# Two transformer blocks on one core: Q and K copied whole from their banks in attention, a loop of four sequences per round, residual and bias summed in TensorE's output bank in the mixer, and row gathers six experts ahead

## The chip, the cores and the metric

The kernel runs on one core of a Trainium2 chip. The time is the device time of one launch in microseconds. A core has TensorE (PE in the profile; it writes only to banks of PSUM), VectorE (DVE), ScalarE (ACT), GpSimd (POOL) and SyncE (SP), each with its own instruction queue, which wait for each other by semaphores; DMAs are issued from SP, ACT and POOL queues.

## What is computed

Sixteen sequences of 512 tokens with 128 channels go through two blocks. The part of the reference that matters:

```python
x = x + _L0_attn_ref(_layernorm(x), W_attn, W_proj)     # 16 heads of 8, causal, ALiBi, softmax
x = x + _L0_ffn_ref(_layernorm(x), ...)                 # expert choice: 8 experts take 256 tokens each
x = x + _L1_attn_ref(_layernorm(x), ...)                # the mixer, below
x = x + _L1_ffn_ref(_layernorm(x), ...)                 # top 2 of 8 experts of width 352

# _L0_attn_ref
scores = jnp.einsum('bhqd,bhkd->bhqk', q, k) * scale + bias
att = jax.nn.softmax(scores, axis=-1)
y = jnp.einsum('bhqk,bhkd->bhqd', att, v)

# _L1_attn_ref (mixer): residual is its own, normalised, input
uv = x @ in_proj_w + in_proj_b
v_local = _dwconv(silu(v), conv_w, conv_b)
h = a * h + ssm_b * vt                                  # a scan over the sequence
out = (u * silu(y_seq)) @ out_proj_w + out_proj_b
h = out + residual
return (h - mu) * rsqrt(var + LN_EPS) * ln_w + ln_b
```

## The kernel before

The stages follow one another: attention, its projection with the router (project), the choice of tokens (choose), expert choice, the mixer, the gate of the second feed-forward part with its dispatch, and the experts. The change touches attention, expert choice and the mixer.

**Attention.** One round of the loop handles one sequence b in four steps `st`, one for each group of four heads. All engines run the same sequence of rounds: two unrolled, a hardware loop (`Fori`) whose body holds two rounds, two unrolled (`steps`, L235 to L248). In a step TensorE follows the list `ORDER`. S0 to S5 are score products for the row maxima (L436 mask, L441 product), into two PSUM pairs `psS`, from which VectorE takes maxima (`mx`, L548); then VectorE splits the maxima in two bf16 parts `mhl` (L556, L558), TensorE turns them (M, L476), ScalarE copies them to `mT` (L574), and SyncE's DMA puts them into `qop` (L283). E0 to E5 are the score products again, with the maxima inside, for the step two before (L455), twelve units into a ring of three banks `psE`; ScalarE takes the exponential of each (`probs`, L619), GpSimd clears the future part (L344). V0 to V3 multiply by the values (L467) into `psY`, which ScalarE copies (`ysb`, L600).

Into these steps the preparation of the next sequence is woven: transposes of its normalised x (X, L379) at step 0, the products for Q and K (L384) in step 0 and for V (W, L387) in step 2, each into the next bank of the same ring (`RING`). Q and K are needed as three bf16 parts that add up to the f32 value. ScalarE writes the high part from the bank (`hi_part`, L582), VectorE subtracts it from the bank into `rest` (`split`, L514), and GpSimd makes the middle and the low part from `rest` (`split_rest`, L335, L337). A bank with Q or K is free for its next use when `rest` is done:

```python
elif kind_ in "QK":
    eng.wait_ge(s_rst, 2 * bb + 3 + (kind_ == "K"))
```

The parts go to HBM (SyncE) and come back spread over partitions into `qop` and `kop` (`place_q`, `place_k`, L223 and L229, from GpSimd's queue).

**Expert choice.** For each of eight experts GpSimd gathers 256 rows with two indirect DMAs (L1142), TensorE turns them (L1191), and goes through two layers (L1204, L1216); VectorE makes the contribution `ctr`, which GpSimd adds to x in HBM with two indirect DMAs (L1157), each pair after the pair before has landed.

**Mixer.** A skewed pipeline over sequences, written with steps s: ScalarE normalises x of s to `xn` (L1463), TensorE turns it (L1435), then multiplies for V and U (L1440, L1443); VectorE does the taps of the convolution (`tap`, L1550) and the scan (L1579) of s-1 and the product `z` (L1592); for b = s-2 TensorE multiplies z by `wout` into `psO` (L1428), GpSimd has made `xo` = `xn` + bias (L1407), VectorE adds both to `ho` (L1560) and takes its statistics (L1566). The chain of eight small operations (L1512 to L1522) serves x of s+1 and h of s-2 together, GpSimd raises to the power -1/2 and makes `shift` (L1384, L1386), and ScalarE writes `hn` from `ho` (L1493).

## Time and profile before

| | us |
|---|---|
| runs, median (lowest to highest of 3) | 1696.02 (1693.43 to 1698.18) |
| profiled execution | 1699.34 |
| its span in the trace | 1697.4 |
| attention, 40 to 690 | 650 |
| expert choice, 870 to 948 | 78 |
| mixer, 948 to 1132 | 184 |

The last three are stretches of the trace, cut by hand where the stage's first and last operations stand. A line of a timeline gives start, duration, engine, line of the kernel, operation, output and input, and in brackets the idle time before it and what ended it.

### The profile page before, as it was taken

The page shows a single profiled execution, that of the slowest core. Times are in us where ns is not written, and L with a number is a line of the kernel's source. Part 1 is how long each engine was busy: PE and PEld are TensorE (multiplying, and loading weights), DVE is VectorE, ACT ScalarE, POOL GpSimd, SP SyncE. Part 2 cuts the span into 40 slices and gives each one's busy share as a digit, 9 for nine tenths or more (in the row PEclk, how much of TensorE's full clock was granted, in tenths as well). Part 3 has the DMA queues.
Part 4 walks back from the last instruction along what each step waited for, and adds up shares of the span by engine and source line. Part 5 has one row for each costly group of instructions (what it writes and reads, how often), then busy time and mean ns, then how long its engine had stood idle before and what let it go on. Part 6 is the DMA issues. An engine that isn't in the chain of part 4 may idle for free. (4 is left out here: it accounts for less than half of the span.)

```text
span 1697.4 us, 34915 instructions
## 1 busy us (share of the span) xinstructions
PE 1208.6 (71%) x9400; PEld 720.5 (42%) x9403; DVE 1140.5 (67%) x3202; ACT 824.4 (49%) x2033; POOL 966.2 (57%) x1007
## 2 busy tenths in 40 slices
PE   2788787888777888585037266617279899899997
PEld 1333333433333433275036033307246565555655
DVE  2878687777766778286743289867766676666664
ACT  1577676666655767111312266633334444444443
POOL 1465465555454653242016388967157777787777
PEclk7899999999989999565558565555579999999999
DMA  4433243333322431362014300300413333333333
GB/s 106 152 83 97 70 110 91 90 88 86 84 68 79 100 101 64 103 219 95 0 57 97 69 25 25 127 7 25 179 28 42 40 41 41 40 41 42 41 40 39
DMA packets 87021, 124.46 MB, mean 73 GB/s; under 512 B 22050, under 2 KB 57826, under 8 KB 82834
## 3 DMA queue, kind: packets, MB, share of 16 engines
q0 software_dynamic: 39712, 44.13, 16.5%
q1 hardware_dynamic: 39170, 65.92, 11.8%
q10 hardware_dynamic: 8032, 12.93, 2.1%
q8 instruction: 73, 1.20, 0.3%
q14 instruction: 34, 0.28, 0.1%
HBM read 65.23 MB, written 57.16 MB: 72 GB/s over the span
## 5 line engine op out<-in xcount | busy, mean ns | idle before, releaser
L548 DVE TENSOR_REDUCE mx<-psS 128x2 f32<-128x768 f32 (+3 forms) x384 | 386.4, 1042 | 164.0 <-PE psS L441 163.5
L619 ACT ACTIVATE probs<-psE 128x512 f32<-128x512 f32 (+2 forms) x768 | 344.6, 523 | 157.5 <-PE psE L455 156.1
L344 POOL TENSOR_SCALAR_AFFINE_SELECT probs<-probs 128x512 f32<-128x512 f32 x256 | 162.3, 643 | 255.0 <-ACT probs L619 254.9
L2038 POOL DMA_INDIRECT out<-ex_y,ex_idx x136 | 219.2, 1612 | 59.0 <-issue 33.8
L455 PE MATMUL psE<-qop,kop 63*128 63x512 bf16 (+3 forms) x1024 | 194.2, 309 | 75.0 <-DVE rest L514 34.8
L467 PE MATMUL psY<-probs,vaug 128*32 128x512 f32 (+3 forms) x2048 | 178.8, 460 | 9.0 <-POOL probs L344 9.0
L2029 POOL DMA_INDIRECT ex_xg<-expert_tab,ex_idx x136 | 134.1, 986 | 60.8 <-issue 38.7
L2096 PE MATMUL ex_psY<-ah_w3s,ex_hT 128*128 (+1 forms) x816 | 127.4, 293 | 26.3 <-DVE ex_y L2022 24.0
L441 PE MATMUL psS<-kop,qop 61*128 61x128 bf16 (+3 forms) x1024 | 140.0, 307 | 0.0
L455 PEld LDWEIGHTS psE<-qop,kop 63*128 63x128 bf16 x1024 | 64.7, 95 | 155.9 <-ACT probs L619 90.5
L436 PE MATMUL psS<-maskq,spread 64*128 64x128 bf16 (+2 forms) x1536 | 114.0, 225 | 21.3 <-DVE mx L548 20.9
L2106 ACT ACTIVATE ex_hT<-ex_psH 128x256 f32<-128x256 f32 x136 | 52.1, 383 | 157.9 <-PE ex_psH L2072 157.9
L2096 PEld LDWEIGHTS ex_psY<-ah_w3s,ex_hT 128*128 128x128 f32 (+1 forms) x816 | 105.3, 196 | 44.2 <-issue 42.7
L436 PEld LDWEIGHTS psS<-maskq,spread 64*128 64x128 bf16 x1536 | 56.6, 96 | 125.1 <-DVE mx L548 88.1
L2078 PE MATMUL ex_psU<-ah_w1s,ex_xT 128*128 x272 | 108.5, 482 | 0.5 <-ACT ex_xT L2117 0.5
L2022 DVE COPY ex_y<-ex_psY 128x128 f32<-128x128 f32 x136 | 39.7, 292 | 100.2 <-issue 51.9
L2079 PE MATMUL ex_psG<-ah_w2s,ex_xT 128*128 x272 | 106.9, 476 | 0.0
L2008 DVE SCALAR_TENSOR_TENSOR ex_h<-ex_psG,ex_w,ex_up 128x352 f32<-128x352 f32 x136 | 79.3, 583 | 38.6 <-ACT ex_w L2113 25.9
L467 PEld LDWEIGHTS psY<-probs,vaug 128*32 128x32 f32 x2048 | 68.1, 113 | 62.5 <-issue 31.2
L2117 ACT ACTIVATE ex_xT<-ex_psX 128x128 f32<-128x128 f32 x136 | 37.7, 277 | 75.8 <-PE ex_psX L2065 73.5
L2072 PE MATMUL ex_psH<-ident,ex_h 128*128 128x128 f32 (+1 forms) x408 | 71.1, 284 | 0.9 <-DVE ex_h L2008 0.9
L1142 POOL DMA_INDIRECT ec_xg<-norm_tab,idx x16 | 15.7, 982 | 93.0 <-POOLq L896 88.5
(318 smaller groups left out, 2549.7 us busy)
## 6 DMA issues: line engine op xcount, KB each, us to landing
y_scr<-ysb SPq DMA_DIRECT2D x64, 256.0 KB, 2.8
qkv_scr<-parts SPq DMA_DIRECT2D x32, 384.0 KB, 3.2
qop<-qkv_scr POOLq DMA_DIRECT2D x30, 192.0 KB, 4.5
kop<-qkv_scr POOLq DMA_DIRECT2D x30, 192.0 KB, 5.6
expert_tab<-table_rows SPq DMA_DIRECT2D x1, 4352.0 KB, 13.5
pj_num<-y_scr SPq DMA_DIRECT2D x16, 256.0 KB
pj_rec<-rec_scr SPq DMA_DIRECT2D x16, 256.0 KB
x_scr<-x_all ACTq DMA_DIRECT2D x16, 256.0 KB, 3.4
```

The costliest lines, as they stand in the source:

```text
L344: pool.affine_select(diag, diag, [[0, HG], [1, P]], ALU.is_ge, 0.0, base=0, channel_multiplier=-1).then_inc(s_msk, 1)
L436: pe.matmul(out[:, :, P * j + lo:w], spread[rows, lo // HALF], maskq[rows, 0:nh, 0:P - lo], start=(lo == 0), stop=False, skip_group_check= ...
L441: mm = pe.matmul(out[:, h, :], half(qop[n], p, ROW_MAX)[:, hh, P * j:P * j + P], half(kop[n], p, ROW_MAX)[:, hh, 0:w], start=False, stop=( ...
L455: mm = pe.matmul(ring_bank(st, u)[:, W[j] * h:W[j] * h + W[j]], half(kop[m], p, ROW_END)[:, hh, P * j:P * j + P], half(qop[m], p, ROW_END) ...
L467: mm = pe.matmul(psY[32 * h:32 * h + 32, P * k:T], vaug[m_v][:, k, HG * e_v + h, :], probs[e_v % 2][k][:, h, :], start=(k == 0), stop=(k = ...
L548: dve.tensor_reduce(out, src, AX, ALU.max).then_inc(s_su, 1)
L619: act.activation(probs[st % 2][j][:, 2 * p + h0:2 * p + h0 + nh, :].rearrange("p h q -> p (h q)"), ring_bank(st, k)[:, 0:nh * W[j]], ACT.E ...
L2029: pool.indirect_dma_start(xg[t % 4][:], None, ytab, bass.IndirectOffsetOnAxis(ap=idx[t % 8][:], axis=0))\
L2038: pool.indirect_dma_start(out, bass.IndirectOffsetOnAxis(ap=idx[t % 8][:], axis=0), y[m][:], None, compute_op=ALU.add).then_inc(s_sc[m], 16)
L2078: pe.matmul(psU[n][:, 0:DE], xT[n][:], flat(w1s[:, e, :]), start=True, stop=True).then_inc(s_g2, 1)
L2079: pe.matmul(psG[n][:, 0:DE], xT[n][:], flat(w2s[:, e, :]), start=True, stop=True).then_inc(s_g, 1)
L2096: i = pe.matmul(psY[:, 0:C], hT[m][0:wd, f], flat(w3s[0:wd, f, e, :]), start=(f == 0), stop=(f == len(FC) - 1))
```

## The change

In attention ScalarE copies Q and K as f32 from the bank into `rest` (`copy_raw`), and the bank is free with that copy (`s_raw`). VectorE then makes the high part from `rest` in SBUF and subtracts it in place. The order within a step changes: M behind E0, V2 and V3 behind E2, Q's product ahead of S2; ScalarE copies `mT` after its second exponential, `ysb` after its sixth; GpSimd makes K's parts later in its step. The loop body holds four rounds in place of two. In expert choice the first six pairs of gathers are issued at once. In the mixer TensorE puts bias (a bf16 product of ones with three bias parts) and residual (`xn` by the unit matrix) into the bank `psO` before z's product is added there; `xo`, `ho` and their additions are gone, and VectorE's statistics and ScalarE's `hn` read the bank.

The core of the diff:

```diff
-        ORDER = ["S0", "E0", "S1", "E1", "M", "V2", "V3", "S2", "E2", "S3", "E3", "S4", "E4", "S5", "E5", "V0", "V1"]
+        ORDER = ["S0", "E0", "M", "S1", "E1", "S2", "E2", "V2", "V3", "S3", "E3", "S4", "E4", "S5", "E5", "V0", "V1"]
...
-                        eng.wait_ge(s_rst, 2 * bb + 3 + (kind_ == "K"))
+                        eng.wait_ge(s_raw, 2 * bb + 3 + (kind_ == "K"))
-            eng.wait_ge(s_rst, 2)
+            eng.wait_ge(s_raw, 2)
...
-            with eng.Fori(1, nb // 2 - 1) as i:
-                for n in range(2):
-                    body(n, 2 * i + n, False)
+            with eng.Fori(0, (nb - 4) // 4) as i:
+                for k in range(4):
+                    body(k % 2, 4 * i + 2 + k, False)
...
-                pool.wait_ge(s_rst, 2 * b + s + 1)
+                pool.wait_ge(s_rst, 4 * b + 2 * s + 2)
...
                     if st == 1 and more:
-                        for k in range(2):
-                            split_rest(b + 1, k)
+                        split_rest(b + 1, 0)
...
                     for j in range(TT):
+                        if st == 1 and more and j == 2:
+                            split_rest(b + 1, 1)
...
-                        if what == "S3" and st == 0 and not last:
+                        if what == "S2" and st == 0 and not last:
...
-            def split(b, s, bank):
-                dve.wait_ge(s_hi, 2 * b + s + 1)
-                if not isinstance(b, int) or b:
-                    dve.wait_ge(s_lo, 2 * b + s - 1)
-                dve.tensor_tensor(rest[s][:], bank[:], parts[s][:, 0], ALU.subtract).then_inc(s_rst, 1)
+            def split(b, s):
+                dve.wait_ge(s_raw, 2 * b + s + 1)
+                if isinstance(b, int) and b == 1:
+                    dve.wait_ge(s_head, 48)
+                elif not isinstance(b, int) or b:
+                    dve.wait_ge(s_pw[s], 16 * b - 16)
+                dve.tensor_copy(parts[s][:, 0], rest[s][:]).then_inc(s_rst, 1)
+                dve.wait_ge(s_rst, 4 * b + 2 * s + 1)
+                dve.tensor_tensor(rest[s][:], rest[s][:], parts[s][:, 0], ALU.subtract).then_inc(s_rst, 1)
             for s in range(2):
-                split(0, s, psE[s])
-                dve.wait_ge(s_rst, s + 1)
+                split(0, s)
+                dve.wait_ge(s_rst, 2 * s + 2)
...
-                if st == 1 and not last:
-                    split(b + 1, 1, ring_bank(0, "K"))
...
                     if k == 3 and st == 0 and not last:
-                        split(b + 1, 0, ring_bank(0, "Q"))
+                        split(b + 1, 0)
+                    if k == 2 and st == 1 and not last:
+                        split(b + 1, 1)
...
-            def hi_part(b, s, use, bank):
+            def copy_raw(b, s, use, bank):
-                if isinstance(b, int) and b == 1:
-                    act.wait_ge(s_head, 48)
-                elif not isinstance(b, int) or b:
-                    act.wait_ge(s_pw[s], 16 * b - 16)
-                act.activation(parts[s][:, 0], bank[:], ACT.Copy).then_inc(s_hi, 1)
+                if not isinstance(b, int) or b:
+                    act.wait_ge(s_lo, 2 * b + s - 1)
+                act.activation(rest[s][:], bank[:], ACT.Copy).then_inc(s_raw, 1)
...
                                        ring_bank(st, k)[:, 0:nh * W[j]], ACT.Exp).then_inc(s_ex, 1)
-                    if k == 3:
-                        if there(G * b + st - 1):
-                            copy_max(b, st, last)
-                        if there(u) and there(u - 1):
-                            copy_y(u - 1, st + 1)
-                    if k == 5 and ahead:
-                        hi_part(b + 1, 0, use_next(b, 1), ring_bank(0, "Q"))
+                    if k == 1 and there(G * b + st - 1):
+                        copy_max(b, st, last)
+                    if k == 3 and ahead:
+                        copy_raw(b + 1, 0, use_next(b, 1), ring_bank(0, "Q"))
+                    if k == 5 and there(u) and there(u - 1):
+                        copy_y(u - 1, st + 1)
                     if k == 9 and ahead:
-                        hi_part(b + 1, 1, use_next(b, 2), ring_bank(0, "K"))
+                        copy_raw(b + 1, 1, use_next(b, 2), ring_bank(0, "K"))
...
-            for e in range(3):
-                gather(e)
+            def gather_next(e):
+                if 3 <= e < E:
+                    pool.wait_ge(s_xg[e % 3], 32 * (e // 3))
+                if e < E:
+                    gather(e)
+            for e in range(AHEAD):
+                gather_next(e)
             for e in range(E):
-                if e + 3 < E:
-                    pool.wait_ge(s_xg[e % 3], 32 * (e // 3 + 1))
-                    gather(e + 3)
+                if e:
+                    gather_next(e + AHEAD - 1)
...
-                if live(s, nb):
-                    pool.wait_ge(s_xn, s + 1)
-                    if not isinstance(s, int) or s >= 2:
-                        pool.wait_ge(s_h, s - 1)
-                    pool.tensor_tensor(xo[n][:], xn[n][:], rows_s[:, 0], ALU.add).then_inc(s_xo, 1)
...
                     pe.wait_ge(s_z, b + 1)
-                    if not isinstance(b, int) or b >= 2:
-                        pe.wait_ge(s_h, b - 1)
                     for t in range(TT):
-                        i = pe.matmul(psO[n][:, P * t:P * t + P], z[n][:, P * t:P * t + P], wout_s[:], start=True, stop=True)
+                        i = pe.matmul(psO[n][:, P * t:P * t + P], z[n][:, P * t:P * t + P], wout_s[:], start=False, stop=(t == TT - 1),
+                                      skip_group_check=True)
                     i.then_inc(s_o, 1)
+                if live(s - 1, nb):
+                    r = s - 1
+                    if isinstance(r, int) and r == 0:
+                        pe.wait_ge(s_bias, 9)
+                    if not isinstance(r, int) or r >= 2:
+                        pe.wait_ge(s_hn, r - 1)
+                    pe.matmul(psO[1 - n][:], ones[:], bias3[:], start=True, stop=False, skip_group_check=True)
+                    for t in range(TT):
+                        i = pe.matmul(psO[1 - n][:, P * t:P * t + P], ident[:], xn[1 - n][:, t], start=False, stop=False, skip_group_check=True)
+                    i.then_inc(s_open, 1)
...
-                        i = act.activation(hn[n][:, t], ho[n][:, t], ACT.Identity, bias=shift[:, u:u + 1], scale=rstd[:, u:u + 1])
+                        i = act.activation(hn[n][:, t], psO[n][:, P * t:P * t + P], ACT.Identity, bias=shift[:, u:u + 1], scale=rstd[:, u:u + 1])
...
+            row = rows_s[0:BROWS, 0].rearrange("p t c -> p (t c)")
+            dve.memset(ones[:], 1.0).then_inc(s_bias, 1)
+            dve.memset(bias3[:], 0.0).then_inc(s_bias, 1)
+            dve.tensor_copy(biashi[:], row).then_inc(s_bias, 1)
+            dve.wait_ge(s_bias, 3)
+            dve.tensor_tensor(biasrest[0][:], row, biashi[:], ALU.subtract).then_inc(s_bias, 1)
+            dve.tensor_copy(bias3[0:1], row[0:1]).then_inc(s_bias, 1)
+            dve.wait_ge(s_bias, 5)
+            dve.tensor_copy(biasmid[:], biasrest[0][:]).then_inc(s_bias, 1)
+            dve.tensor_copy(bias3[32:33], biasrest[0][32:33]).then_inc(s_bias, 1)
+            dve.wait_ge(s_bias, 7)
+            dve.tensor_tensor(biasrest[1][:], biasrest[0][:], biasmid[:], ALU.subtract).then_inc(s_bias, 1)
+            dve.wait_ge(s_bias, 8)
+            dve.tensor_copy(bias3[64:65], biasrest[1][64:65]).then_inc(s_bias, 1)
...
                 if live(s - 2, nb):
-                    b = s - 2
-                    dve.wait_ge(s_o, b + 1)
-                    dve.wait_ge(s_xo, b + 1)
-                    if not isinstance(b, int) or b >= 2:
-                        dve.wait_ge(s_hn, b - 1)
-                    dve.tensor_tensor(ho[n][:], psO[n][:].rearrange("p (t c) -> p t c", t=TT), xo[n][:], ALU.add).then_inc(s_h, 1)
-                tap(2)
-                if live(s - 2, nb):
-                    dve.wait_ge(s_h, s - 1)
+                    dve.wait_ge(s_o, s - 1)
                     for t in range(TT):
-                        i = dve.bn_stats(stats[:, TT + t], ho[n][:, t])
+                        i = dve.bn_stats(stats[:, TT + t], psO[n][:, P * t:P * t + P])
                     i.then_inc(s_hs, 1)
+                tap(2)
```

How the order moves, at three places. First, attention's second round, step 0, on TensorE, from E0 on (L455 or L456 is E, L476 or L477 is M, L436/L437 with L441/L442 is S, L384/L385 is Q's product, L467/L468 V2 and V3). Before:

```order
L455 MATMUL psE<-qop,kop 128x512 x2
L436 MATMUL psS<-maskq,spread 128x2x128 x2
L436 MATMUL psS<-maskq,spread 128x2x64 x2
L441 MATMUL psS<-kop,qop 128x256 x4
L455 MATMUL psE<-qop,kop 128x512 x2
L476 MATMUL psE<-identb,mhl 8x128 x4
L467 MATMUL psY<-probs_2,vaug 32x256 x4
L467 MATMUL psY<-probs_3,vaug 32x128 x4
L436 MATMUL psS<-maskq,spread 128x128 x2
```

Now:

```order
L456 MATMUL psE<-qop,kop 128x512 x2
L477 MATMUL psE<-identb,mhl 8x128 x4
L437 MATMUL psS<-maskq,spread 128x2x128 x2
L437 MATMUL psS<-maskq,spread 128x2x64 x2
L442 MATMUL psS<-kop,qop 128x256 x4
L456 MATMUL psE<-qop,kop 128x512 x2
L385 MATMUL psE<-xT,wT 128x512
L437 MATMUL psS<-maskq,spread 128x128 x2
L437 MATMUL psS<-maskq,spread 128x64 x2
L442 MATMUL psS<-kop,qop 128x384 x2
L456 MATMUL psE<-qop,kop 128x384 x2
L468 MATMUL psY<-probs_2,vaug 32x256 x4
```

M moved ahead of S1 and E1, Q's product ahead of S2, V2 and V3 behind E2.

VectorE in steps 0 and 1 of the same round (L548 or L551 takes maxima, L556/L558 or L561/L563 make `mhl`, L514, or L517 with L519, is the split). Before:

```order
L548 TENSOR_REDUCE mx<-psS 128x4 x2
L548 TENSOR_REDUCE mx<-psS 128x2 x2
L514 TENSOR_TENSOR rest<-psE,parts 128x512
L548 TENSOR_REDUCE mx<-psS 128x2 x2
L556 CAST mhl<-mx 128x8x2
L558 TENSOR_TENSOR mhl<-mx,mhl 128x8x2
L514 TENSOR_TENSOR rest<-psE,parts 128x512
```

Now:

```order
L551 TENSOR_REDUCE mx<-psS 128x4 x2
L551 TENSOR_REDUCE mx<-psS 128x2 x2
L517 CAST parts<-rest 128x512
L519 TENSOR_TENSOR rest<-rest,parts 128x512
L551 TENSOR_REDUCE mx<-psS 128x2 x2
L561 CAST mhl<-mx 128x8x2
L563 TENSOR_TENSOR mhl<-mx,mhl 128x8x2
L551 TENSOR_REDUCE mx<-psS 128x4 x2
L551 TENSOR_REDUCE mx<-psS 128x2
```

Each split has become a cast and a subtraction that read SBUF alone, and K's has moved from the start of step 1 to behind its third maximum.

Second, TensorE in an unrolled step of the mixer (`mx_psX` is the transposes, `mx_psV` and `mx_psU` the input products). Before:

```order
L1428 MATMUL mx_psO<-mx_wout,mx_z 128x128 x4
L1435 MATMUL mx_psX<-ident,mx_xn 128x128 x4
L1440 MATMUL mx_psV<-mx_xT,mx_win 128x512
L1443 MATMUL mx_psU<-mx_xT,mx_win 128x512
L1428 MATMUL mx_psO<-mx_wout,mx_z 128x128 x4
```

Now:

```order
L1432 MATMUL mx_psO<-mx_wout,mx_z 128x128 x4
L1442 MATMUL mx_psO<-mx_bias_rows,mx_ones 128x512
L1444 MATMUL mx_psO<-mx_xn,ident 128x128 x4
L1451 MATMUL mx_psX<-ident,mx_xn 128x128 x4
L1456 MATMUL mx_psV<-mx_xT,mx_win 128x512
L1459 MATMUL mx_psU<-mx_xT,mx_win 128x512
```

The bias and the residual of s-1 stand between the output product of s-2 and the transposes of s.

Third, GpSimd's queue in expert choice, gathers into `ec_xg` and scatters into `x_scr`. Before:

```order
L1142 DMA ec_xg<-norm_tab,idx 128x128 x8
L1157 DMA x_scr<-ec_ctr,idx 8192x128 x2
L1142 DMA ec_xg<-norm_tab,idx 128x128 x2
L1157 DMA x_scr<-ec_ctr,idx 8192x128 x2
L1142 DMA ec_xg<-norm_tab,idx 128x128 x2
L1157 DMA x_scr<-ec_ctr,idx 8192x128 x2
```

Now:

```order
L1145 DMA ec_xg<-norm_tab,idx 128x128 x12
L1164 DMA x_scr<-ec_ctr,idx 8192x128 x2
L1145 DMA ec_xg<-norm_tab,idx 128x128 x2
L1164 DMA x_scr<-ec_ctr,idx 8192x128 x2
L1145 DMA ec_xg<-norm_tab,idx 128x128 x2
L1164 DMA x_scr<-ec_ctr,idx 8192x128 x12
```

Six pairs of gathers come first, and two of the other pairs stand ahead of a scatter instead of four.

## Rows read from the trace of the kernel before

**Rows 1.** The page: its span line and its lines of 40 slices.
```profile
span 1697.4 us, 34915 instructions
...
PEclk7899999999989999565558565555579999999999
```

**Rows 2.** Stretches: length, busy PE PEld DVE ACT POOL (count), clock, DMA, GB/s.
```profile
40.00:690.00 650.00, 524.56 (x6097) 245.42 (x6100) 484.08 (x739) 430.44 (x955) 341.66 (x509) 0.95 0.35 91
...
948.00:1132.00 184.00, 100.41 (x256) 50.88 (x256) 140.01 (x393) 105.15 (x210) 139.53 (x121) 0.59 0.17 55
```

**Rows 3.** Timeline of TensorE: start us, duration us, what [idle before <-releaser].
```profile
239.88 0.47 PE L455 MATMUL psE<-qop,kop 63*128 63x256 bf16 x4 [1.19 <-DVE rest L514]
...
245.24 0.47 PE L455 MATMUL psE<-qop,kop 63*128 63x512 bf16 x2 [1.29 <-DVE rest L514]
...
252.92 0.38 PE L455 MATMUL psE<-qop,kop 63*128 63x512 bf16 x2
...
273.22 0.65 PE L379 MATMUL psE<-ident,xn 128*128 128x128 f32 x4 [2.87 <-issue]
```

**Rows 4.** Timeline of ScalarE in the same round of attention.
```profile
241.44 0.60 ACT L582 ACTIVATE parts<-psE 128x512 bf16<-128x512 f32 x1
...
245.66 2.06 ACT L619 ACTIVATE probs<-psE 128x512 f32<-128x512 f32 x4 [3.04 <-PE psE L455]
```

**Rows 5.** Timelines of VectorE and GpSimd in the same round.
```profile
243.42 1.16 DVE L558 TENSOR_TENSOR mhl<-mx,mhl 128x16 bf16<-128x16 f32 x1
...
243.29 1.26 POOL L335 TENSOR_TENSOR parts<-rest,zeros 128x512 bf16<-128x512 f32 x1
```

**Rows 6.** Timeline of VectorE in the first round: cast and subtraction, SBUF to SBUF.
```profile
13.91 0.43 DVE L519 CAST parts<-rest 128x512 bf16<-128x512 f32 x1
...
14.37 0.69 DVE L521 TENSOR_TENSOR parts<-rest,parts 128x512 bf16<-128x512 f32 x1
```

**Rows 7.** Groups by line: xcount, busy us, mean ns, idle before, releasers.
```profile
L455 PE MATMUL psE<-qop,kop 63*128 63x512 bf16 (+3 forms) x1024 | 194.2, 309 | 75.0 <-DVE rest L514 34.8 <-ACT probs L619 20.3 <-DMA qop<-mT 12.8
...
L379 PE MATMUL psE<-ident,xn 128*128 128x128 f32 x60 | 11.8, 329 | 35.6 <-DMA kop<-qkv_scr 23.0 <-issue 12.6
...
L1493 ACT ACTIVATE mx_hn<-mx_ho,mx_nrm_shift,mx_nrm_rstd 128x128 f32<-128x128 f32 x64 | 26.3, 482 | 9.4 <-POOL mx_nrm_shift L1386 9.4
```

**Rows 8.** Timeline of GpSimd in expert choice.
```profile
891.70 1.63 POOL L1157 DMA_INDIRECT x_scr<-ec_ctr,idx  x1 [10.29 <-DVE ec_ctr L1288]
...
899.26 1.62 POOL L1157 DMA_INDIRECT x_scr<-ec_ctr,idx  x1 [1.44 <-DMA x_scr<-ec_ctr,idx]
...
936.94 1.55 POOL L1157 DMA_INDIRECT x_scr<-ec_ctr,idx  x1 [2.44 <-DMA x_scr<-ec_ctr,idx]
...
942.84 1.55 POOL L1157 DMA_INDIRECT x_scr<-ec_ctr,idx  x1 [2.48 <-DMA x_scr<-ec_ctr,idx]
```

**Rows 9.** The view of waits, 870 to 950 us: what, total us, times, longest.
```profile
PE ec_psX L1191 <- DMA ec_xg<-norm_tab,idx: 25.4, 5, 13.4
```

**Rows 10.** Timeline of the mixer: its first tap, then two steps.
```profile
968.64 0.75 DVE L1550 SCALAR_TENSOR_TENSOR mx_c<-mx_vs,mx_prm,mx_c 128x512 f32<-128x512 f32 x1 [5.41 <-ACT mx_c L1479]
...
1031.68 0.20 POOL L1386 TENSOR_TENSOR mx_nrm_shift<-mx_nrm_minus_mean,mx_nrm_rstd 128x8 f32<-128x8 f32 x1
...
1032.59 2.07 PE L1428 MATMUL mx_psO<-mx_wout,mx_z 128*128 128x128 f32 x8 [1.54 <-DVE mx_z L1592]
...
1034.78 0.69 DVE L1560 TENSOR_TENSOR mx_ho<-mx_psO,mx_xo 128x512 f32<-128x512 f32 x1 [1.12 <-PE mx_psO L1428]
...
1035.23 1.11 PE L1435 MATMUL mx_psX<-ident,mx_xn 128*128 128x128 f32 x4 [0.58 <-ACT mx_xn L1463]
...
1042.30 1.16 PE L1428 MATMUL mx_psO<-mx_wout,mx_z 128*128 128x128 f32 x8 [1.71 <-DVE mx_z L1592]
...
1045.02 1.12 PE L1435 MATMUL mx_psX<-ident,mx_xn 128*128 128x128 f32 x4 [1.57 <-ACT mx_xn L1463]
...
1051.00 0.20 POOL L1386 TENSOR_TENSOR mx_nrm_shift<-mx_nrm_minus_mean,mx_nrm_rstd 128x8 f32<-128x8 f32 x1
```

More of the change, by code:

```diff
@@ L167, in attention @@
             for what in ORDER:
-                before = {(0, "S3"): "Q", (0, "S5"): "K", (2, "S4"): "W"}
+                before = {(0, "S2"): "Q", (0, "S5"): "K", (2, "S4"): "W"}
                 if (st, what) in before:
@@ L1106, in expert_choice @@
     SCORE = 6
+    AHEAD = 6
     with ExitStack() as ctx:
@@ L1334, in mixer @@
             "a", "b", "c", "minus_mean", "var", "veps", "rstd", "shift"))
-        xn, xT, vs, c0, vl, hs, dv, ys, z, xo, ho, hn = (two(n, s) for n, s in (
+        xn, xT, vs, c0, vl, hs, dv, ys, z, hn = (two(n, s) for n, s in (
             ("xn", [P, TT, C]), ("xT", [P, T]), ("vs", [P, T + 2]), ("c0", [P, T]), ("vl", [P, T]), ("hs", [P, T]),
-            ("dv", [P, T]), ("ys", [P, T]), ("z", [P, T]), ("xo", [P, TT, C]), ("ho", [P, TT, C]), ("hn", [P, TT, C])))
+            ("dv", [P, T]), ("ys", [P, T]), ("z", [P, T]), ("hn", [P, TT, C])))
+        BROWS = 65
+        bias3, biashi, biasmid = (sb("bias_" + n, [BROWS, T], BF16) for n in ("rows", "hi", "mid"))
+        biasrest = [sb(f"bias_rest{k}", [BROWS, T], F32) for k in range(2)]
+        ones = sb("ones", [BROWS, P], BF16)
         t1, t2 = sb("t1", [P, TT, C], F32), sb("t2", [P, TT, C], F32)
@@ L1343, in mixer @@
         psO = [ps("psO0"), ps("psO1")]
[L1344 to L1345 removed]
+        s_w, s_p, s_set, s_xs, s_hs, s_n, s_r, s_xn, s_tr, s_xT, s_uv, s_vs, s_c0, s_c, s_dv, s_y, s_ys, s_z, s_o, s_open, \
+            s_bias, s_hn, s_t1, s_x3, s_pre, s_v, s_ahead = (sem(n) for n in (
                 "weights", "powers", "set", "x_stats", "h_stats", "chain", "shift", "xn_ready", "turned", "xT_ready", "uv_ready",
[L1347 removed]
+                "v_ready", "conv0", "conv", "dv_ready", "y_ready", "silu_y", "z_ready", "out_ready", "residual_in_psum", "bias_parts",
                 "hn_ready", "t1_ready", "x3_ready", "prepared", "v_product", "loaded_ahead"))
```

9 lines of the change are left out of this document (3 added, 6 removed).

## The prediction

> **What bounds the kernel now.** I read the page first: no engine is full over the span of 1697.4 us, and TensorE's clock falls behind the first 16 slices [rows 1]. So each stage has to be priced by itself. The stretches show attention at 650 us and the mixer at 184 us; in attention no engine is busy above 81% (TensorE 525 of 650, VectorE 484, ScalarE 430), in the mixer VectorE and GpSimd have 140 of 184 [rows 2]. Both are stages of hand-offs, where only a wait on the chain counts. The experts stage behind them is not touched.
>
> In attention I took one round (one sequence, four steps) and looked at TensorE's waits. It stops twice, 1.19 us and 1.29 us, on VectorE's `rest` [rows 3]: the ring bank with Q, then that with K, is kept until VectorE has subtracted, though ScalarE's copy of K was over at 242.04 and TensorE could have gone on at 243.95. ScalarE then sits idle 3.04 us for the next scores [rows 4]. A plain step, E0 at 245.24 to E0 at 252.92, takes 7.7 us [rows 3]. Over the kernel TensorE's waits there are 34.8 us on `rest` and 12.8 us on the small DMA that brings the row maxima into `qop` [rows 7].
>
> **The loop.** Before, six iterations with five branches back; after, three with two. At a branch back the first transposes stand 2.87 us in "issue" [rows 3]; their whole issue idle is 12.6 us [rows 7], 2.5 for each of the five. All engines branch together, so nothing covers it. Three less give **8 us** (7.6 to 8.6). That the body is twice as long has no price in this trace: the unrolled code ahead of the loop pays nothing of the kind.
>
> **Banks freed by the copy.** ScalarE now copies Q and K whole (same form, 0.60 us [rows 4]) and the bank is free then. The two waits go: 34.8 us over 15 rounds, 2.3 a round [rows 7]. VectorE pays: where it did one subtraction from a bank (0.69 us, as `ho` [rows 10]) it now does a cast of 0.43 and a subtraction of 0.69 [rows 6], 0.43 more, twice in 15 rounds, 13 us if all were on the path. Part is not: in the step of the K split, VectorE has a hole ahead of the fourth maximum, since V2 and V3 now stand between S2 and S3. In Q's step it has none; there the projection itself, moved ahead of S2, also makes S2 later. Then the port: with `parts` being made on GpSimd (243.29 to 244.55), VectorE's subtraction of 16 elements takes 1.16 us [rows 5]. The new split has both operands in SBUF, the old one read a PSUM bank. One such block in each round would be 17 us. The Trainium skill (SBUF — State Buffer, Who interferes with whom) says that a VectorE operation with two SBUF inputs, or in a two-port mode, waits out a GpSimd operation that reads SBUF; it would add blocks by GpSimd's selects to each split, and by that rule alone the gain here would be near the low end. From rows: 34.8 less 13 less 17 is 5, and with neither 35. I take the middle, **20 us**, 1.3 a round.
>
> **The maxima earlier.** M stands behind E0 now, and its copy behind two exponentials in place of four, which is 1.0 us earlier (four take 2.06 [rows 4]). The transfer of `mT` starts that much sooner. Of 12.8 us [rows 7] I take **5**; bounds 0 and 12.8. M ahead of S1 and E1 also means that TensorE stands at it if VectorE's `mhl` is late. That is the fourth rival. V2, V3 and ScalarE's copy of Y move too, at nothing: TensorE and ScalarE do the same work in the step, and the chain (exponentials to unit 8, E5, V0 and V1, S0, E0) holds neither in another place.
>
> **Gathers six ahead.** TensorE waits 25.4 us for gathered rows, 13.4 of it the first time [rows 9], which stays. GpSimd issues pairs 4 to 7 between scatters. With six pairs ahead, experts no longer wait and the scatters bind: each pair waits until the one before has landed, 5.90 us at the end, 7.56 for the second pair [rows 8]. The last pair could start at 899.26 + 6 x 5.90 = 934.7 in place of 942.84, 8.2 us earlier; at 7.56 each nothing is won. I take **7 us** (0 to 8). The first scatter at 891.70 doesn't move: GpSimd stands idle 10.29 us ahead of it after eight gathers, room for four more.
>
> **The mixer.** Its cycle goes over two steps: shift (end 1031.88), `xn`, transposes, V, the product z, the output matmuls, `ho`, statistics, shift (end 1051.20): 19.32 us, 9.7 a step [rows 10]. Off it go VectorE's 0.69 and GpSimd's `xo`, which is covered itself but, as in attention, can block VectorE's operations; half of one block of 1.16 [rows 5], 0.6, is my guess for it. New on TensorE, between output matmuls and transposes: four f32 matmuls with `ident` like the output group (1.16 us at the 2.4 GHz clock, 2.07 at 1.2) and one bf16 matmul of 512 columns, 0.2 or 0.4 (from the pair of 0.38 in [rows 3]). At 2.4 GHz that is 1.36 us, and the hole until the transposes is 1.56 (1043.46 to 1045.02): hidden. At 1.2 GHz it is 2.5, and the hole is 0.57: the transposes come 1.9 late. The new group also waits until ScalarE has read the bank (`hn` of s-3), and transposes, V and U are queued behind it; `hn` follows the shift (1031.88) with four operations of 0.48 [rows 7], over at 1033.8 at the latest, before TensorE is through the output group at 1.2 GHz and 0.3 after it at 2.4: nothing. Per cycle -1.3 or +0.6, eight cycles: -10 or +5. Bounds: +15 if nothing is saved; -20 if the fuller TensorE keeps the high clock and the groups on the cycle shrink as 2.07 to 1.16 did. The granted clock of the stage is 0.59 [rows 2], mostly the low level. The Trainium skill (TensorE: Matmul & The Clock Gate, What's actually happening) calls the low clock the default and says that activity releases it; that speaks for the -10. I take **-6**. The eleven new operations on `bias3`, seven of them 512 columns wide at 0.4 to 0.7 us [rows 6], come to some 4 us, and stand ahead of the first tap, which waits 5.41 us for ScalarE [rows 10]: 0; without that cover 4.
>
> **The sum.** 8 + 20 + 5 + 7 + 6 = 46 us. The profiled execution took 1699.3 us, 1.9 more than its span, so 1653.3; it lies 3.3 above the median of the runs, 1696.0, which gives **1650 us**.
>
> **Rivals.**
> 1. *VectorE takes the waits' place in attention (0.14).* Both splits and `mhl` are blocked by GpSimd, the banks' gain shrinks to 5 and that of the maxima to 0: 46 - 15 - 5 = 26, **1670 us**. For it: the 1.16 us. Against: VectorE is busy 484 of 650 us.
> 2. *The mixer stays at 1.2 GHz and TensorE's new group delays the transposes (0.10).* +5 to +15 for -6: **1666 us**. For it the clock of 0.59; against it, such a TensorE would be busy nearly all the time.
> 3. *Better than forecast (0.11).* All 34.8 us come back and the mixer runs at the high clock: 1650 - 15 - 14, **1621 us**.
> 4. *Slower than before (0.05).* M, now ahead of S1 and E1, waits in each of some 60 steps for `mhl`. It decides from 46/60 = 0.8 us a step on; at the 1.16 us of [rows 5] plus the chain behind it, 60 x 1.2 = 72: **1722 us**. Against it: the block here stands where GpSimd makes `parts`, in one step of four, and E0's exponentials cover some of it.
> 5. *The change does nothing in its stages (0.05):* scatters bind at 7.56, VectorE fills the waits, the mixer's two effects cancel, and the branch gains are lost to fetching the longer body: **1696 us**.
>
> **How the numbers follow.** The forecast has 0.55 and a range of its own of 1635 to 1663. To hold 8 in 10 the range goes up to rivals 1 and 2 and down most of the way to 3: **1623 to 1674**. A change of this kernel under 0.3% (5 us) can't be told from none. Faster holds the forecast and rivals 1 to 3: 0.90; rival 5 is the same but for 0.01 of it, which with rival 4 makes slower 0.06; same is 0.04.
>
> **What would show it.** Right: no TensorE wait on `rest`; step 0 and step 1 of a round together 1.5 to 2 us shorter; two branches back; waits on `mT` under 8 us; the last scatter pair 44 us after the first (51 before); mixer steps of 9.0 to 9.4 us with a clock above 0.59. Wrong: `mhl` or the split's cast standing 0.6 us and more behind GpSimd, TensorE waiting at M, transposes of the mixer late behind the residual, or VectorE's maxima taking over as what ScalarE's idle time ends on.

## The result, and where the 41 us are

The changed kernel takes 1656.13 us in the median of four runs (1654.99 to 1662.06), the kernel before 1697.1 on the same chip: a ratio of 0.9754, with an interval of 0.9721 to 0.9787. That is 41 us less. The profiled execution spans 1655.3 us (before 1697.4 [rows 1]). Its page, the span line and TensorE's granted clock in 40 slices:

```profile
span 1655.3 us, 35150 instructions
...
PEclk7899999999999999665558678755599999999999
```

In the slices of the mixer, behind the middle of the line, there are now 7 and 8 where 5 and 6 stood. The stretches show it: attention, the mixer, and the mixer again from its first `shift` to its last (length, busy time of PE, PEld, DVE, ACT and POOL, clock, DMA share, GB/s):

```profile
40.00:665.00 625.00, 518.53 (x6091) 233.41 (x6089) 504.59 (x769) 442.66 (x952) 340.17 (x508) 0.96 0.36 93
915.70:1090.00 174.30, 99.96 (x400) 65.88 (x400) 129.28 (x388) 101.76 (x211) 114.69 (x108) 0.75 0.18 58
928.00:1082.00 154.00, 99.96 (x400) 65.88 (x400) 125.71 (x366) 99.71 (x205) 108.28 (x97) 0.79 0.15 53
```

Attention is 25 us shorter and VectorE is busier in it, 505 us for 484 [rows 2]; in the mixer VectorE has 11 us less to do and the clock is 0.75 for 0.59 [rows 2]. Since the stages follow one another, their marks divide the gain. The first gather of expert choice starts at 845.89 (before 871.53): 25.6 us from attention. From there to the last scatter it is 66.5 us (before 73.2): 6.7. From the first `shift` of the mixer to the last, 153.9 (before 163.4): 9.5. The way from the last scatter to that first `shift` gives 0.6, and all behind the mixer takes 0.4 more.

The groups of the changed kernel that answer to [rows 7], and the new waits beside them:

```profile
L456 PE MATMUL psE<-qop,kop 63*128 63x512 bf16 (+3 forms) x1024 | 185.3, 306 | 53.4 <-ACT probs L622 28.3 <-DMA qop<-mT 21.1
...
L519 DVE TENSOR_TENSOR rest<-rest,parts 128x512 f32<-128x512 f32 x32 | 26.8, 838 | 1.1
...
L477 PE MATMUL psE<-identb,mhl 128*8 128x128 bf16 x256 | 25.8, 226 | 20.4 <-DVE mhl L563 10.1 <-ACT probs L622 9.0 <-ACT xT L572 0.4
...
L517 DVE CAST parts<-rest 128x512 bf16<-128x512 f32 x32 | 13.3, 417 | 4.5 <-ACT rest L585 4.5
...
L380 PE MATMUL psE<-ident,xn 128*128 128x128 f32 x60 | 10.8, 306 | 30.0 <-DMA kop<-qkv_scr 23.9 <-issue 6.1
```

M in the kernel before:

```profile
L476 PE MATMUL psE<-identb,mhl 128*8 128x128 bf16 x256 | 25.8, 225 | 7.0 <-ACT probs L619 2.7
```

The 34.8 us on `rest` are gone. But the waits on the transfer of the maxima went up, 12.8 to 21.1, those on `probs` from 20.3 to 28.3, and TensorE stands 20.4 us at M (L477), where it stood 7.0; 10.1 of them are for VectorE's `mhl`. Q's subtraction is blocked in 14 of 15 rounds (1.00 to 1.04 us, 0.69 unblocked); K's (0.69) and the casts (0.42) are not.

To see in which step the time went I took the start of VectorE's cast of `mhl`, one at the end of each step, and added up the distances over the 15 rounds. "Step 0" is the distance from the cast of the step 3 ahead, and holds the branch back.

| sums over 15 rounds, us | step 1 | step 2 | step 3 | step 0 | all |
|---|---|---|---|---|---|
| before | 138.7 | 130.8 | 159.9 | 170.3 | 599.7 |
| changed | 124.8 | 126.8 | 162.0 | 161.4 | 575.0 |
| loop4_alone | 138.6 | 130.2 | 166.7 | 161.6 | 597.2 |
| after_loop2 | 125.1 | 127.5 | 165.3 | 173.1 | 591.1 |
| banks_alone | 130.8 | 138.0 | 156.4 | 166.8 | 592.0 |
| maxima_late | 118.9 | 124.5 | 177.4 | 166.1 | 586.9 |
| subtract_twice | 140.6 | 128.8 | 163.7 | 174.6 | 607.6 |
| place_late | 125.4 | 126.7 | 153.4 | 174.6 | 580.2 |
| place_norm | 125.1 | 127.5 | 152.7 | 168.1 | 573.4 |
| place_norm_maxima_late | 118.8 | 125.2 | 154.8 | 164.5 | 563.3 |

The gain sits in step 1 (13.9 us), step 0 (8.9) and step 2 (4.0); step 3 gave nothing. Each row is one profile. How far it can be trusted is seen from kernels below that have the same attention: the sums of the changed kernel, no_residual and xo_back are 575.0, 581.0 and 576.2 us, those of wait_behind_x and write_back_late 552.4 and 560.2. Steps 1 and 2 agree within 1 us in them; step 3 differs by up to 3.5 us, and step 0 by up to 8.4. In every kernel step 3 of round 10 takes 17 to 20 us: TensorE stands 6 to 10 us there, while GpSimd shows "issue" at its placement of K (10.65 us before, 9.72 in the changed kernel).

### The profile page after: what moved, and what is told of

Same layout as the page of the kernel before. It is cut to its first block and busy times, and to the rows that moved or that the text cites. A ratio compares the mean times of both kernels' runs of the same rounds, so it can differ in the third digit from the quotient of the medians.

```text
span 1655.3 us, 35150 instructions
## 1 busy us (share of the span) xinstructions
PE 1193.6 (72%) x9544; PEld 716.0 (43%) x9547; DVE 1149.6 (69%) x3227; ACT 834.3 (50%) x2033; POOL 939.0 (57%) x991
## 3 DMA queue, kind: packets, MB, share of 16 engines
q8 instruction: 68, 1.11, 0.3%
## 5 line engine op out<-in xcount | busy, mean ns | idle before, releaser
L551 DVE TENSOR_REDUCE mx<-psS 128x2 f32<-128x768 f32 (+3 forms) x384 | 387.3, 1040 | 119.1 <-PE psS L442 117.9
L622 ACT ACTIVATE probs<-psE 128x512 f32<-128x512 f32 (+2 forms) x768 | 352.1, 524 | 127.8 <-PE psE L456 124.4
L456 PE MATMUL psE<-qop,kop 63*128 63x512 bf16 (+3 forms) x1024 | 185.3, 306 | 53.4 <-ACT probs L622 28.3
L468 PE MATMUL psY<-probs,vaug 128*32 128x512 f32 (+3 forms) x2048 | 167.8, 446 | 9.2 <-POOL probs L344 9.2
L2120 PE MATMUL ex_psY<-ah_w3s,ex_hT 128*128 (+1 forms) x816 | 127.9, 294 | 25.9 <-DVE ex_y L2046 23.4
L442 PE MATMUL psS<-kop,qop 61*128 61x128 bf16 (+3 forms) x1024 | 140.1, 306 | 0.0
L437 PE MATMUL psS<-maskq,spread 64*128 64x128 bf16 (+2 forms) x1536 | 114.6, 225 | 16.9 <-DVE mx L551 16.6
L456 PEld LDWEIGHTS psE<-qop,kop 63*128 63x128 bf16 x1024 | 61.7, 95 | 121.9 <-ACT probs L622 86.3
L437 PEld LDWEIGHTS psS<-maskq,spread 64*128 64x128 bf16 x1536 | 54.3, 95 | 118.2 <-DVE mx L551 54.6
L468 PEld LDWEIGHTS psY<-probs,vaug 128*32 128x32 f32 x2048 | 54.1, 110 | 81.1 <-issue 44.3
L2135 ACT ACTIVATE ex_up<-ex_psU 128x352 f32<-128x352 f32 x136 | 63.0, 463 | 11.4 <-PE ex_psU L2102 5.1
```

Of the source, the lines that this page charges most:

```text
L437: pe.matmul(out[:, :, P * j + lo:w], spread[rows, lo // HALF], maskq[rows, 0:nh, 0:P - lo], start=(lo == 0), stop=False, skip_group_check= ...
L442: mm = pe.matmul(out[:, h, :], half(qop[n], p, ROW_MAX)[:, hh, P * j:P * j + P], half(kop[n], p, ROW_MAX)[:, hh, 0:w], start=False, stop=( ...
L456: mm = pe.matmul(ring_bank(st, u)[:, W[j] * h:W[j] * h + W[j]], half(kop[m], p, ROW_END)[:, hh, P * j:P * j + P], half(qop[m], p, ROW_END) ...
L468: mm = pe.matmul(psY[32 * h:32 * h + 32, P * k:T], vaug[m_v][:, k, HG * e_v + h, :], probs[e_v % 2][k][:, h, :], start=(k == 0), stop=(k = ...
L551: dve.tensor_reduce(out, src, AX, ALU.max).then_inc(s_su, 1)
L622: act.activation(probs[st % 2][j][:, 2 * p + h0:2 * p + h0 + nh, :].rearrange("p h q -> p (h q)"), ring_bank(st, k)[:, 0:nh * W[j]], ACT.E ...
```

## The experiments

**The loop: loop4_alone and after_loop2.** The first is the kernel before with

```diff
-            with eng.Fori(1, nb // 2 - 1) as i:
-                for n in range(2):
-                    body(n, 2 * i + n, False)
+            with eng.Fori(0, (nb - 4) // 4) as i:
+                for k in range(4):
+                    body(k % 2, 4 * i + 2 + k, False)
```

and the second is the changed kernel with this undone.

> The kernel before, with the body of attention's loop made four rounds long (three iterations, two branches back) and nothing else changed. Theory A (each branch back costs what it shows as issue, and nothing is paid for the longer body): 8 us less than before, ratio 0.995, and two issue waits of 2.3 to 2.9 us in place of five. Rival B (the longer body costs instruction fetches elsewhere): 0 to 3 us less, with new unexplained idle time inside rounds. Rival C (a branch costs more than its wait shows, 3.5 us of a step): 11 to 12 us less.

> The changed kernel with the loop body of two rounds as before (six iterations, five branches back). Theory A: 8 us more than the changed kernel, 1664. Rival B (longer body pays elsewhere): 1656 to 1659. Rival C (3.5 us for each of three branches): 1667 to 1668.

loop4_alone: 1686.0 us (10 runs), ratio 0.9937 (0.9915 to 0.9958), 7 to 14 us less than before. after_loop2: 1670.9 us, ratio 0.9828 (0.9785 to 0.9870), 15 more than the changed kernel. (Each ratio is to the kernel before, timed beside it. By the two ratios the 15 are 13; such differences of two medians below are good to a few us.) Step 0 lost 8.7 us and gained 11.7, three branches each time: 2.9 to 3.9 us for one, where its wait shows 2.3 to 2.9. The profile of loop4_alone is of its slowest run, 1697.4 us, so that little can be read from its other steps. The plainest reading is in after_loop2: its five steps 0 with a branch take 14.0 to 14.1 us, most of the others 10.3 to 10.8. loop4_alone lies between A and C (3.5 us a branch), after_loop2 at C or above it; B, with less than 3 us, is out.

**The banks alone: banks_alone.** The kernel before, with `copy_raw`, the early release and VectorE's cast and subtraction in SBUF, and no other order:

```diff
-                        eng.wait_ge(s_rst, 2 * bb + 3 + (kind_ == "K"))
+                        eng.wait_ge(s_raw, 2 * bb + 3 + (kind_ == "K"))
...
-                dve.tensor_tensor(rest[s][:], bank[:], parts[s][:, 0], ALU.subtract).then_inc(s_rst, 1)
+                dve.tensor_copy(parts[s][:, 0], rest[s][:]).then_inc(s_rst, 1)
+                dve.wait_ge(s_rst, 4 * b + 2 * s + 1)
+                dve.tensor_tensor(rest[s][:], rest[s][:], parts[s][:, 0], ALU.subtract).then_inc(s_rst, 1)
...
-                act.activation(parts[s][:, 0], bank[:], ACT.Copy).then_inc(s_hi, 1)
+                act.activation(rest[s][:], bank[:], ACT.Copy).then_inc(s_raw, 1)
```

> The kernel before with one part of the change: ScalarE copies Q and K as f32 into rest, the bank is free then, VectorE makes the high part from rest and subtracts in place. The order of each engine, the loop of two rounds, the gathers and the mixer are as before. Theory A (the term of 20 us, bounds 5 and 35): the waits on rest (34.8 us) are gone, 20 us less, near 1675. Rival B (VectorE and the transfer of the maxima take most of it: over the whole change steps 0 and 1 of a round gave back 1.2 us, and step 2 nothing): 8 to 15 us less, 1680 to 1688.

1689.1 us (12 runs), ratio 0.9954 (0.9931 to 0.9976): 7 us less, 4 to 12. The part that I had priced at 20 gives 7 alone. Its groups:

```profile
L436 PE MATMUL psS<-maskq,spread 64*128 64x128 bf16 (+2 forms) x1536 | 113.7, 226 | 47.7 <-DVE mx L552 47.0
...
L518 DVE TENSOR_TENSOR rest<-rest,parts 128x512 f32<-128x512 f32 x32 | 26.6, 832 | 1.1
L516 DVE CAST parts<-rest 128x512 bf16<-128x512 f32 x32 | 26.1, 815 | 4.9 <-ACT rest L584 4.9
```

TensorE does not wait for `rest` any more, but 47.0 us for VectorE's maxima; before it was 20.9. K's split stands at the start of step 1 there, while GpSimd makes the parts of Q, and K's cast takes 1.31 us for 0.42; 0.82 is the mean over Q's and K's. (The Trainium skill, SBUF — State Buffer, Who interferes with whom, names two kinds of VectorE operations that wait out GpSimd: those with two SBUF inputs and those in a two-port mode. K's casts have one input; that they wait too, 1.31 us for 0.42, agrees with the second.) And one thing more, in TensorE's timeline of the third round:

```profile
127.43 0.26 PE L436 MATMUL psS<-maskq,spread 64*128 64x128 bf16 x4 [1.11 <-DVE mx L552]
...
128.56 0.26 PE L436 MATMUL psS<-maskq,spread 64*128 64x128 bf16 x4 [0.54 <-DVE mx L552]
...
129.42 0.26 PE L436 MATMUL psS<-maskq,spread 64*128 64x128 bf16 x4 [0.28 <-DVE mx L552]
...
131.23 2.71 PE L467 MATMUL psY<-probs,vaug 128*32 128x512 f32 x16
```

The sixteen matmuls of V0 and V1 take 1.71 us elsewhere. Here they take 2.71, and the stretches around them show the clock:

```profile
129.00:131.00 2.00, 1.66 (x22) 0.70 (x20) 2.00 (x3) 1.61 (x4) 1.57 (x3) 0.72 0.96 314
131.00:134.00 3.00, 3.00 (x26) 0.74 (x25) 1.84 (x4) 0.96 (x3) 2.59 (x5) 0.62 0.51 165
134.00:137.00 3.00, 2.82 (x48) 1.67 (x46) 1.82 (x2) 2.43 (x6) 2.05 (x5) 1.00 0.86 148
```

Behind the short waits on VectorE the granted clock is 0.62 for three us, so mostly at its low level of 1.2 GHz, and then 1.00 again. These three waits stand in 12 rounds, and in 8 of them the clock falls and the V group is slow (6.3 us); why not in the other four is open. Eleven V groups of this kernel are slow, together 10.5 us over their 1.71; three are before (4.2 us), one in the changed kernel (1.2). So the order matters: the changed one puts K's split behind the third maximum and past GpSimd's parts of Q, and the changed kernel's step 1 and step 2 are 6.0 and 11.2 us shorter than those of banks_alone. (M's place is changed between the two as well, and maxima_late below shows that this is no part of it, since M late makes step 1 shorter yet. The moves of K's split, of Q's product and of V2 and V3 were not tried apart.)

What the order wins there it loses again. after_loop2 is banks_alone plus the new order and the early maxima, as far as attention goes. Its steps 1 and 2 are 5.7 and 10.5 us shorter than those of banks_alone, its steps 3 and 0 are 8.9 and 6.3 us longer, and all 15 rounds take 591.1 us for 592.0. Step 3 is where TensorE waits for the transfer of the maxima (23.4 us in after_loop2, 12.1 in banks_alone).

**The maxima: maxima_late.** The changed kernel with M back:

```diff
-        ORDER = ["S0", "E0", "M", "S1", "E1", "S2", "E2", "V2", "V3",
+        ORDER = ["S0", "E0", "S1", "E1", "M", "S2", "E2", "V2", "V3",
...
-                    if k == 1 and there(G * b + st - 1):
+                    if k == 3 and there(G * b + st - 1):
                         copy_max(b, st, last)
```

> The changed kernel with the transposes of the maxima (M) back behind S1 and E1 and their copy back behind ScalarE's fourth exponential. V2, V3 and the raw copies stay. Theory A (the early place of M is worth what was predicted): 5 us more, 1661. Rival B (the early place costs: TensorE stood 20.4 us at M, and the waits on the transfer of the maxima grew anyway): 5 to 12 us less, 1644 to 1651, with M's waits under 8 us. Rival C (no matter): within 3 us.

1668.7 us, ratio 0.9836 (0.9793 to 0.9879): 13 us more than the changed kernel. Both mechanisms are real and the table separates them. Steps 1 and 2 get 8.2 us shorter without the waits at M; step 3 gets 15.4 and step 0 4.7 longer (the last is within what profiles differ by), since the transfer of the maxima lands later still:

```profile
L456 PE MATMUL psE<-qop,kop 63*128 63x512 bf16 (+3 forms) x1024 | 199.4, 317 | 61.6 <-DMA qop<-mT 32.1 <-ACT probs L622 21.8
```

**VectorE's share: subtract_twice.** The changed kernel with

```diff
+                dve.tensor_tensor(parts[s][:, 1], rest[s][:], parts[s][:, 0], ALU.subtract)
                 dve.tensor_tensor(rest[s][:], rest[s][:], parts[s][:, 0], ALU.subtract).then_inc(s_rst, 1)
```

> The changed kernel with one more subtraction of 512 elements in each of VectorE's splits (rest minus the high part into the tile of the middle part, which GpSimd overwrites), to price VectorE's share of the split: 30 times 0.7 to 1.0 us of work. Theory A (VectorE's time in steps 0 and 1 is on the path): 20 to 30 us more than the changed kernel, 1676 to 1686. Rival B (it lies in holes): within 8 us of it.

1689.0 us (10 runs), 33 more: 1.1 us for each of 30 added subtractions, more than the 0.84 us that the added line takes. TensorE's wait for `mhl` at M went from 10.1 to 31.1 us. Step 0 is 13.2 us longer and step 1 15.8, 0.9 and 1.1 a round: VectorE's time in both is on the path in full.

**What holds up the maxima's transfer: place_late, place_norm, place_norm_maxima_late.** In the changed kernel TensorE waits at the start of step 3 in 13 rounds. One of them (queues of SP and POOL beside TensorE; rows of three engines, in order of time):

```profile
173.58 1.33 SPq L283 DMA_DIRECT2D qop<-mT  x2
...
173.96 2.00 POOL L223 DMA_DIRECT2D qop<-qkv_scr  x4
...
176.55 1.70 POOL L229 DMA_DIRECT2D kop<-qkv_scr  x3
...
182.34 0.50 PE L456 MATMUL psE<-qop,kop 63*128 63x512 bf16 x2 [1.74 <-DMA qop<-mT]
```

The transfer, twice 4 KB, is issued from 173.58 on, and TensorE's wait for it ends at 182.3; beside it run the placements of Q and K, twelve DMAs with 1.5 MB, issued from 172.84 to 180.48. place_late issues them one select later:

```diff
-                        for p in range(2):
-                            place_q(pool, 1 - b % 2, s_op, p)
...
                         clear_future(u, j)
+                        if st == 2 and more and j == 0:
...
+                            for p in range(2):
+                                place_q(pool, 1 - b % 2, s_op, p)
-                        if st == 2 and more and j < 2:
+                        if st == 2 and more and 1 <= j < 3:
```

> The changed kernel with GpSimd's DMAs that place Q and K for the next sequence put one select later (Q behind the first select of step 2, K behind the second and the third). In the changed kernel TensorE waits 1.1 to 2.6 us for the transfer of the maxima at the start of step 3 in nearly every round (21.1 us in 13 waits), and that transfer is issued 0.4 us ahead of the big placement transfers. Theory A (the small transfer is held up by the placement transfers): the wait falls under 0.5 us a round, 10 to 20 us less, unless the next round then waits for its Q and K. Rival B (the delay is not from the placements): the waits stay, the time is the same or longer.

The waits on `mT` fell from 21.1 us to nothing, as theory A says, and step 3 is 8.6 us shorter; yet the kernel takes 1660.0 us (ratio 0.9779, 0.9740 to 0.9818), no less than the changed one. In step 3 TensorE now stands for VectorE:

```profile
186.11 0.26 PE L437 MATMUL psS<-maskq,spread 64*128 64x128 bf16 x4 [1.65 <-DVE mx L551]
```

because VectorE's normalisation waits for GpSimd's factors, which stand behind the placements. This wait is there in 14 rounds, and in four of them the V group behind it is slow, as in banks_alone (5.0 us; 9.4 in all seven slow groups of this kernel). Step 0 is 13.2 us longer. place_norm moves the normalisation two maxima later:

```diff
-                    if k == 3 and ahead:
+                    if k == 5 and ahead:
                         norm_apply(b + 2, use_next(b, 0) + 1)
```

> place_late, and VectorE's normalisation of the sequence after next moved from ahead of its fourth maximum in step 3 to ahead of its sixth. In place_late the waits on the transfer of the maxima were gone, but TensorE stood 1.65 us in each round at step 3's products for VectorE, which stood behind GpSimd's factors, which stood behind the placements. Theory A (that is all that ate the gain): 1.65 us in some 14 rounds come back, 20 to 24 us less than place_late, near 1637. Rival B (another wait is next: the next round's Q and K land too late, or VectorE stands 1.6 us later at the sixth maximum instead): 0 to 8 us less.

1651.2 us (ratio 0.9763, 0.9714 to 0.9812): 9 less than place_late by the medians, 3 by the ratios, and not clearly less than the changed kernel. The slow V groups in the rounds are gone, and step 0 gets 6.5 us back, no more than such sums differ by. The theory's 20 to 24 do not come: rival B. The next wait is at the round's start, where X stands 40.6 us for K in all, 23.9 in the changed kernel. The first, in the kernel's start, takes 22.8 and all of the 23.9; the rest is in eleven later rounds:

```profile
153.55 1.11 PE L380 MATMUL psE<-ident,xn 128*128 128x128 f32 x4 [3.32 <-DMA kop<-qkv_scr]
```

With M late as well:

> place_norm with the transposes of the maxima back behind S1 and E1. maxima_late was 0.55 us a round shorter in steps 0 and 1 (its waits at M were 6 us for 20) and lost 1.3 us a round to the transfer of the maxima. Theory A (the transfer is no longer held up, so only the gain is left): 6 to 9 us less than place_norm. Rival B (the transfer now comes too late by itself): 0 to 10 us more.

1643.1 us, ratio 0.9701 (0.9652 to 0.9750): 8 less than place_norm, 10 by the table, as theory A says. The place of M is right or wrong only together with that of the placements.

**wait_behind_x** is that kernel with TensorE's wait for the placed Q and K behind X.

> place_norm_maxima_late with TensorE's wait for the placed Q and K moved from ahead of the transposes of x (X) in step 0 to ahead of the score products that need them. In that kernel X stood 1.4 to 2.6 us for the placement of K in 9 of 14 rounds. Theory A (X and ScalarE's copy of xT are done in the wait): 0.7 us in each of these rounds, 6 to 9 us less, near 1635. Rival B (the score products wait just as long and all hangs on them): 0 to 3 us less.

1647.6 us, ratio 0.9723 (0.9689 to 0.9758): nothing gained that can be measured. The 15 rounds are shorter, 552.4 us for 563.3 (560.2 in write_back_late, with the same attention), but the start is 9 to 10 us later (TensorE's first score products, and ScalarE's queue):

```profile
49.87 0.50 PE L437 MATMUL psS<-maskq,spread 64*128 64x256 bf16 x4 [26.15 <-DMA kop<-qkv_scr]
...
23.76 3.91 ACTq L612 DMA_DIRECT2D x_all<-x  x7
```

ScalarE issues seven loads of 512 KB behind its first copy of xT. That copy started at 40.58 and does so at 23.75 now, and so the loads run beside the first placement of K, for which TensorE's wait ends at 49.9 in place of 39.4. That the loads are the cause was not tested: holding them back was not tried.

**The mixer: xo_back, no_residual, write_back_late.** xo_back puts GpSimd's addition back, into a tile that nobody reads:

```diff
+                if live(s, nb):
+                    pool.wait_ge(s_xn, s + 1)
+                    pool.tensor_tensor(spare[:], xn[n][:], rows_s[:, 0], ALU.add)
```

> The changed kernel with GpSimd's addition of xn and bias put back into the mixer, into a tile that nobody reads. Theory A (half of a block of 1.2 us a cycle, as guessed): 5 us more in the mixer, 155 to 158. Rival B (GpSimd's instruction was on the path: the factors and the write-back come 1.3 us later in each of 16 steps): up to 20 us more. Rival C: nothing.

161.3 us from the first `shift` to the last, 1668.4 in all (ratio 0.9850, 0.9820 to 0.9880). Eight profiles with the changed kernel's mixer (its own and those of seven experiments) show 149.0 to 153.9 there, with 151.0 in the middle. So GpSimd's one instruction a step (1.58 us long) costs some 10 us over the 16 steps, 0.6 a step, without being waited for. For the same operations VectorE is busy 139 us there and 126 in the changed kernel. Its first tap shows how (blocked 1.29, unblocked 0.74 us; 907 ns on average in the changed kernel):

```profile
L1585 DVE SCALAR_TENSOR_TENSOR mx_c<-mx_vs,mx_prm,mx_c 128x512 f32<-128x512 f32 x16 | 18.2, 1139 | 1.9 <-ACT mx_c L1499 1.9
```

That GpSimd's own later work, up to 20 us by rival B, has a part in the 10 is not excluded. And the stage is only 2 us shorter than before (163.4), though VectorE's 16 additions to `ho` are gone.

no_residual leaves out the four matmuls of the residual, so its output lacks the mixer's residual:

> The changed kernel without the four matmuls that put the residual into the mixer's output bank (the bias matmul stays, so that the output lacks the normalised input of the mixer). From the first shift to the last the mixer took 163.4 and 164.9 us in the two profiles with the old mixer, and 153.9, 151.4, 149.0 and 150.4 in four with the new one. Theory A (the new group on TensorE is hidden behind xn, and keeps TensorE's granted clock up): the same 149 to 154 us, or more if the clock falls back. Rival B (the group delays the transposes): 1 us per two steps less, 141 to 146.

155.1 us, 1659.9 in all (ratio 0.9783, 0.9745 to 0.9822; the whole time cannot be told from the changed kernel's). With less to do for TensorE the stage is no shorter. The stretches from first to last `shift` of the kernel before, no_residual, maxima_late and xo_back:

```profile
961.00:1125.00 164.00, 100.41 (x256) 50.88 (x256) 136.61 (x373) 103.44 (x206) 133.84 (x115) 0.60 0.15 49
```

```profile
934.00:1089.00 155.00, 99.83 (x272) 51.22 (x272) 120.47 (x366) 99.57 (x205) 106.35 (x97) 0.63 0.16 52
```

```profile
942.00:1091.00 149.00, 90.16 (x400) 61.70 (x400) 126.35 (x366) 100.01 (x205) 108.55 (x97) 0.86 0.16 54
```

```profile
931.00:1092.00 161.00, 100.96 (x400) 67.49 (x400) 139.15 (x364) 100.79 (x205) 133.16 (x112) 0.79 0.15 50
```

Without the residual group the clock is 0.63, with it 0.79 to 0.86, and TensorE's 400 matmuls take 90 us (in maxima_late) to 101, where 272 took 100. Before, 256 took 100 at 0.60. The Trainium skill (TensorE: Matmul & The Clock Gate, What's actually happening) says that activity releases the clock; this trace agrees, 0.63 to 0.86 by more matmuls.

write_back_late is wait_behind_x with GpSimd's last addition one step later, `t1` and `t2` twice.

> wait_behind_x, and in the mixer GpSimd adds the result into x one step later, behind the factors, with t1 and t2 twice. In the changed kernel VectorE's first small operation (0.73 us on average for 0.17 unblocked) stands behind that addition. Theory A: the mixer 0.5 us a step shorter, 8 us, 141 to 145 us from the first shift to the last. Rival B (the addition now blocks the taps of the convolution instead): no change in the mixer, or longer.

1643.3 us, ratio 0.9690 (0.9657 to 0.9723), and 148.1 us in the mixer. The first small operation is down from 0.62 to 0.39 us on average, the third from 0.39 to 0.16; the two taps are up from 0.94 and 0.85 to 1.11 and 1.00: the block has moved, and of 8 us at most 1 to 3 are seen, no more than the new mixer varies by. This one stays inconclusive.

## Why the prediction held, step by step

The forecast was 1650 us; 1656.13 was measured. Its terms were 8 + 20 + 5 + 7 + 6 = 46, and the sum came nearer than its parts, in part by luck. By stage it had 33 us for attention, 7 for expert choice and 6 for the mixer; the marks show 25.6, 6.7 and 9.5. Within attention the misses are larger: the loop gave more than its 8, and banks and maxima, priced at 25 together, gave 8.6 in the step sums (599.7 to 591.1 us, before to after_loop2). From the run times of after_loop2, 24 to 29 us under the kernel before, less 6.7 for expert choice and 12 for its mixer, it is 6 to 10.

- *The loop, 8.* Right, and a little small: 8.7 and 11.7 us by the step sums, 9 and 15 by the medians. A branch costs 3 to 4 us, not the 2.5 of its wait.
- *Banks freed by the copy, 20.* The waits went as said; the size was wrong for this part alone, 7 us (4 to 12). "VectorE pays" was the right worry and under-priced: the maxima took 26 us of TensorE's waits in return, and in the old order the clock fell behind them. "Part is not" on the path was wrong for the work itself: an added subtraction costs step 1, with its supposed hole, as much as step 0. The order got no term of its own; it wins 16 us in steps 1 and 2 and loses 15 in steps 3 and 0. Rival 1 is what banks_alone does.
- *The maxima earlier, 5.* 12 to 13 us in the changed kernel, at the upper bound of 12.8; with the placements late it is 8 to 10 the other way. And the sign that I named for it was wrong: the waits on `mT` rose to 21.1 us; without the early M they are 32.1. place_late shows that the placements hold the transfer up. Why the waits are longer than before is not shown; they are 12.1 us in banks_alone, and 19.3 in loop4_alone, where nothing but the loop was changed.
- *M ahead of S1 and E1 waits for `mhl` (rival 4).* It does: TensorE stands 20.4 us at M, 10.1 of them for `mhl`, and steps 1 and 2 lose 8 by the step sums: the right place, a tenth of the price.
- *Gathers six ahead, 7.* The last scatter pair starts 44.3 us after the first (866.25 to 910.55; 51.1 before): 6.8 us. The named sign was 44.
- *The mixer, 6.* 9.5 to 14 us; the steps are 9.0 us on average, as named. The clock rose (0.60 to 0.79 and up to 0.86), and the removed GpSimd addition is worth about 10 where half a block a cycle, 5, was guessed. The 0.69 us of VectorE's addition, 5.5 over eight cycles, cannot be seen beside it. Rival 2 had the wrong sign: the group on TensorE is what keeps the clock up. The new operations on `bias3` are nine, not eleven; they take 3.8 us and are covered, as said.

Of the signs, "steps 0 and 1 of a round 1.5 to 2 us shorter" came out at 1.5 (22.8 us over 15 rounds), but with the loop's 8.7 to 11.7 us in it; without them step 1 is 0.93 us shorter per round and step 0 about nothing. And one of the signs of being wrong, TensorE waiting at M, was there.

## What to carry to other kernels

A wait that is removed from one engine can come back at the engine that took over the work: price that engine's next operation, not only the one that waited. Where a small transfer feeds the chain, look at what bulk traffic is issued in the microseconds around it; and move an early producer and the traffic together, since each alone can lose. An instruction that nobody waits for can still cost a good part of its length (0.6 of 1.58 us here) through the engine that it blocks. And check a sum by its stages before taking a near total for a right account.
